# Cross-attention scores read from 32 partitions, and a PSUM copy put ahead of a square root, in a two-layer gated cross-attention and mixture-of-experts kernel

## What is computed

```python
q = _heads(nx @ W_sq + b_sq, B)              # self-attention, 16 heads of 8
...
so = _merge(_attn(q, k, v), B) @ W_so + b_so
x = x + so
nx = _ln(x, g_ln2, b_ln2)
q = _heads(nx @ W_cq + b_cq, B)              # cross-attention
k = _heads(img @ W_ck + b_ck, B)             # img has 77 rows
v = _heads(img @ W_cv + b_cv, B)
co = _merge(_attn(q, k, v), B) @ W_co + b_co
```

## Time and profile before

| | |
|---|---|
| median of 3 runs | 495.39 us (492.77, 495.39, 497.32) |
| the profiled execution | 495.81 us |
| its span, first to last instruction | 494.0 us |
| mean granted TensorE clock | 0.854 of 2.4 GHz |
| busy: PE, DVE, ACT, POOL | 357.9, 269.0, 203.0, 106.1 us |
| the seam and the cross-attention | about 265 to 335 us of the span |

### The profile page before, as it was taken

The page is one execution under the profiler, slowest core; times in us unless marked ns, Lnnn a source line. Parts: engine busy times, 40 slices in busy tenths (PEclk is TensorE's granted clock), DMA queues, the critical chain, the costliest instruction groups (busy, mean ns, idle before and its releaser), DMA issues.

```text
span 494.0 us, 5895 instructions
## 1 busy us (share of the span) xinstructions
PE 357.9 (72%) x2097; PEld 215.4 (44%) x2099; DVE 269.0 (54%) x687; ACT 203.0 (41%) x323; POOL 106.1 (21%) x144
## 2 busy tenths in 40 slices
PE   1987601995058899999997899878738986779800
PEld 1766501894023323333323485634724334569800
DVE  5235500231475998888813586444697457511366
ACT  2121200331022167777795486746333555651100
POOL 2000077001752531111110000000000356310173
PEclk9999555898567799999999699999958989899955
DMA  4692013011227564000000000009994663201132
GB/s 109 185 317 60 0 53 104 22 44 41 58 72 191 121 182 105 1 2 3 1 3 0 0 1 1 1 8 369 328 290 161 213 214 98 72 1 48 44 68 58
DMA packets 33977, 45.09 MB, mean 91 GB/s; under 512 B 5057, under 2 KB 19720, under 8 KB 33948
## 3 DMA queue, kind: packets, MB, share of 16 engines
q1 hardware_dynamic: 31132, 37.40, 25.8%
q0 software_dynamic: 2816, 7.31, 5.5%
HBM read 31.92 MB, written 12.62 MB: 90 GB/s over the span
## 4 chain that ended last, share of the span: by engine, by line
PE 56%; DVE 14%; POOL 8%; issue 8%; ACT 7%; DMA 6%; SPq 1%; POOLq 0%; DVEq 0%; ACTq 0%
PE ps L1289 8%; PE ps L1486 6%; PE ps L1474 5%; PE ps L1457 5%; POOL R L500 5%; PE ps L1765 4%; DVE mcol L1108 4%; PE ps L1724 3%; PE ps L1404 3%; PE ps L1416 3%; PE ps L1578 3%; POOL disp_d L495 2%; DMA R<-h_d,srow 2%; PE ps L1626 1%; PE ps L1587 1%
## 5 line engine op out<-in xcount | busy, mean ns | idle before, releaser
L1108 DVE TENSOR_REDUCE mcol<-ps 128x1 f32<-128x512 f32 x128 | 80.3, 683 | 6.8 <-PE ps L1457 6.5
L665 ACT ACTIVATE R<-ps 128x1024 f32<-128x1024 f32 x64 | 62.5, 1020 | 25.3 <-PE ps L1474 24.4
L1289 PE MATMUL ps<-ident,R 128*77 128x128 f32 (+1 forms) x216 | 32.4, 290 | 27.5 <-DMA R<-disp_d 24.7
L1457 PE MATMUL ps<-R 72*128 72x512 bf16 x128 | 47.0, 399 | 1.2 <-DVE mcol L1108 0.2
L500 POOL DMA_INDIRECT R<-y_d,grow x32 | 30.4, 951 | 73.5 <-DMA y_d<-R 64.3
L1289 PEld LDWEIGHTS ps<-ident,R 128*77 128x77 f32 (+1 forms) x216 | 25.3, 151 | 44.5 <-DMA R<-disp_d 25.1
L1474 PE MATMUL ps<-R 75*128 75x512 bf16 x128 | 37.6, 379 | 0.3 <-ACT R L665 0.2
L1486 PE MATMUL ps<-R,vaug 128*9 128x512 f32 x256 | 33.5, 595 | 0.6 <-ACT R L665 0.6
L557 POOL DMA_INDIRECT R<-h_d,srow x16 | 16.1, 1007 | 82.4 <-DMA h_d<-ff 74.0
L1289 PE MATMUL ps<-ident,xn 128*128 128x128 f32 x48 | 12.8, 406 | 28.7 <-issue 18.0
L1457 PEld LDWEIGHTS ps<-R 72*128 72x128 bf16 x128 | 12.8, 100 | 36.1 <-DVE mcol L1108 24.5
(11 more groups left out here) (306 smaller groups left out, 670.0 us busy)
## 6 DMA issues: line engine op xcount, KB each, us to landing
R<-in_L_ffn_W_dram SPq DMA_DIRECT2D x1, 6144.0 KB, 19.7
h_d<-R SPq DMA_DIRECT2D x12, 256.0 KB, 3.0
q_d<-R SPq DMA_DIRECT2D x24, 96.0 KB, 2.2
R<-k_d SPq DMA_DIRECT2D x24, 96.0 KB
R<-q_d SPq DMA_DIRECT2D x8, 288.0 KB
R<-in_L_ffn_w_dram SPq DMA_DIRECT2D x1, 2048.0 KB, 11.8
h_d<-ff SPq DMA_DIRECT2D x6, 256.0 KB, 2.9
y_d<-R SPq DMA_DIRECT2D x24, 44.0 KB
```

The costliest lines, as they stand in the source:

```text
L665: s.activation(probs[idx % 4], ps[:, 2 * (idx % 2):2 * (idx % 2) + 2, :].rearrange("p b t -> p (b t)"), ACT.Exp, scale=QK_SCALE).then_inc( ...
L1108: v.tensor_reduce(mcol[:, u, col:col + 1], bank(ring_bank("row", n)), AX.X, ALU.max).then_inc(s1_max, 1)
L1289: return m.transpose(dst, src, ident[0:k, 0:k])
L1457: m.matmul(bank(ring_bank("row", n)), Q9[0:KQ, b, h, t * P:(t + 1) * P], K9[0:KQ, b, h, :], start=True, stop=True).then_inc(s1_mm, 1)
```

## The change

ACT copies the transposed attention of batch 1 before the square root of batch 0 instead of behind it. And each of the score matmuls reads only the 32 partitions on which its four heads lie, in the weights (`qcT`) and in the moving operand (`kbd`): partitions 0 to 31 and 32 to 63 for the two matmuls of an even unit, 64 to 95 and 96 to 127 for those of an odd one. Since `kbd` is zero on the other partitions for these heads, the sums are the same. Outputs, banks, semaphores and the number of instructions stay as they were; the lines from 1577 on move down by up to two.

```diff
@@ ScalarE, after the self-attention
             evac_attnT(0, 0)
+            evac_attnT(0, 1)
             std_of(3, 1, [0])
-            evac_attnT(0, 1)
 
             evac_xT(3, V_LN2, [0])
             std_of(3, 1, [1])
@@ TensorE, cross_scores(un)
                 for j in range(2):
                     h = 8 * half + 4 * j
-                    ins = m.matmul(ps[:, 2 * (un % 2) + j, 0:4 * J], qcT[:, t * P:(t + 1) * P],
-                                   kbd[:, t // TB, h:h + 4, :].rearrange("p h j -> p (h j)"), start=True, stop=True)
+                    rows = slice(HD * h, HD * h + 32)
+                    ins = m.matmul(ps[:, 2 * (un % 2) + j, 0:4 * J], qcT[rows, t * P:(t + 1) * P],
+                                   kbd[rows, t // TB, h:h + 4, :].rearrange("p h j -> p (h j)"), start=True, stop=True)
                 ins.then_inc(c_mm, 1)
```

## The result

| | before | after |
|---|---|---|
| median, us | 494.08 (4 executions, 492.61 to 497.32) | **510.86** (4 executions, 507.80 to 512.87) |
| profiled execution, us (span) | 495.81 (494.0) | 512.16 (510.3) |
| mean granted clock of the profiled execution | 0.854 | 0.809 |

The changed kernel is slower: ratio 1.0325, with its 95% interval 1.0243 to 1.0407 (the two medians alone give 1.034). The forecast was 492.1 us. Where a kernel's executions fall into two groups, both are given with their counts, since these groups are what is studied.

What follows compares the result with a forecast made beforehand. PE was taken to bound the steady rounds, with DVE and ACT close behind. Gains 0.85 + 0.73 + 0.36 + 1.2 + 0.4 = 3.5 us gave 492.1 us; its own range 490.9 to 493.4, with rivals 489.4 to 495.4.

Steps and rivals of the forecast that it cites:

- The seam: 265 to 279 us, ahead of the loop: copying before the square root gains 0.85 us at the second W_cq product.
- drain behind the table load: Rival at ACT's square root: a drain follows the table load and loses 1.4 of the 3.5 us, 493.7; chance 0.03.
- The score group: Loop scores: a unit's four pieces on two row groups fill about 0.78 us instead of 1.20, rounds 1.74.
- The staggered rival: Scores: second group's first piece waits for first group's second; three streams, round 2.00 us, total 495.3; chance 0.12.
- the serial one: Rival in the scores: pieces on different row groups don't overlap; round 2.27 us, total 498.5; chance 0.08.
- Seven steady rounds: Loop, unit 0's transposes to unit 7's: each round 0.17 us shorter, 1.2 us gained.
- the clock rises later: Rival in the loop: one or two rounds at 1.2 GHz, 1.4 us more each; 493.7 to 495.0; chance 0.14.
- Unit 0's scores: First scores, at the low clock: 1.33 us on the chain instead of 2.06, gain 0.73.
- Unit 2's: Scores between unit 0's subtraction and its transposes: 0.94 us instead of 1.30, gain 0.36.
- The value rounds: Loop from unit 8 on: chain runs through value matmuls, transposes and ACT's copies, so rounds keep their old length.
- A shift of the whole tail is passed on: Everything behind the loop is bound by data, not a clock of its own, so earlier gains reach the end.
- the clock doesn't fall: Rival ahead of the loop: the earlier projection splits the idle stretch, clock stays 2.4 GHz; 490.8 us; chance 0.15.

Runs made afterwards that it cites:

- after_warm: Changed kernel plus 22 unused full-array bf16 matmuls where PE would stand idle before the loop and ahead of unit 2; 489.58 us, 0.9886.
- hybrid: Changed kernel with the scores of units 0 to 5 on all 128 partitions, the rest on 32; 492.28 us, 0.9986.
- loop_fill: Changed kernel plus four unused full-array matmuls in each of the loop's first three rounds; 497.00 us, 1.0077.
- scores_only: Changed kernel with the attnT copy back behind the square root, scores on 32 partitions; eight executions 509.71 to 515.45 us, four 492.24 to 495.08.
- seam_only: Changed kernel with scores back on 128 partitions, only the attnT copy moved; 495.92 us, 1.0052.
- switch_only: Kernel with only the copy moved, plus a one-column matmul on 32 partitions ahead of each unit's 128-partition scores; 496.30 us, 1.0053.

## Why the prediction was wrong

**The seam was right.** Times less the entry's 0.31: the root at 269.52, 0.09 behind 269.43, where 0.05 was forecast; no drain behind the table load (268.53 + 1.28, then 269.83), so that rival falls; the first `xT` at 271.66, forecast 271.6; the gap ahead of line 1138 gone; the second W_cq product 0.84 earlier, forecast 0.85.

**The score group was right at the high clock.** Four pieces fill 0.79 us (forecast 0.78), a round is 1.74 (1.74), the transposes behind are 1.10 (1.10). The staggered rival (round 2.00) and the serial one (2.27) fall: `after_warm`, `hybrid` and `loop_fill` all show 1.74.

**The step that failed** is the one under the steady rounds, "Seven steady rounds, from unit 0's transposes to unit 7's: 7 x 0.17 = 1.2", with the rounds behind it. It priced them at the high clock. In place of a gain of 0.17, each round took 1.34 us more than before, 3.25 instead of 1.91. The rival "the clock rises later" named this and sized it well: 1.4 us a round over its high-clock price, where 3.25 - 1.74 = 1.51 came. But I let it last one or two rounds with a chance of 0.14; it lasted to the last scores. I gave no reason for that bound, only that before PE ran without a break from 277.13 and had the high clock back for unit 2. In the changed kernel PE ran without a break from 281.73, and the clock stayed down. What I took from the earlier trace rows was that a full PE row brings the clock back; what these rows showed was at most that a full row of matmuls on 128 partitions does. All matmuls of that stretch are on 128 partitions, so the two could not be told apart there, and I gave that unknown no bound of its own. The range ended at 495.4 for that reason.

The Trainium skill (TensorE: Matmul & The Clock Gate, What's actually happening) says that a gate between the clock's source and the array is set by how busy PE has been of late. This trace does not agree, if busy is what PE's row of the profile shows: 61.98 of 64.60 us at 0.50, and 11.00 of 11.00 us at 1.00 in `loop_fill`.

**What the other steps came to.** Unit 0's scores, which the sum had priced at the low clock, took 1.35 us on the chain, forecast 1.33. Unit 2's were priced at the high clock and came at the low one: 1.40 instead of 1.30, a loss of 0.10 where the sum had a gain of 0.36. The value rounds were forecast to keep their length, as bound by ACT and values; at the low clock PE bound them, and they took 6.12 instead of 3.87. "A shift of the whole tail is passed on" did not hold either: 19.5 us at the end of the scores became 16.3 at the end of the span. The rival "the clock doesn't fall" did not happen: it fell at 271.4. The one mechanism that I had on the slower side, pieces one after the other, was not the one that came.

**What stays open.** Why `scores_only` had a high mean clock in four of 12 executions and the full change in none of ten: no trace of the four exists. What moves the clock at a given moment: the same instructions in the seam had 0.50 from 271.7 to 275.1 us in `hybrid`, from 272.3 to 279.0 in `seam_only`, and from 271.4 on, past the first scores, in the changed kernel, so no window of one trace settles it; the counts of executions carry the argument. Which property of the narrow scores matters, that is, the partitions or how much of the array works at a time. And why the moved copy by itself shows no gain in the median.

## What to carry to other kernels

Before a matmul is cut to fewer partitions, look at whether PE's granted clock is low where it starts: if it is, the narrow matmuls may not bring it back for a long time (54 to 82 us in the traces here), and all of PE's work there runs at half the clock, also what was not touched. If narrow matmuls are worth having, let full-array work go first (the first six units here, which took away the loss but showed no gain), or fill PE's pauses with it (0.8 to 1.1% gained, together with the moved copy), and read the granted clock in windows, beside PE's busy time, before believing any sum. A sum made of durations at 2.4 GHz needs a rival in which its whole stretch runs at 1.2.

## What was not expected of the hardware

- PE at 1.2 GHz for 64.6 us while busy for 61.98 of them, with scores on 32 of 128 partitions between transposes on all of them; on 64 partitions likewise (44.25 of 46.00 us, and low until 355.6 us). In `scores_only` it came back at 325.3 us in the middle of such scores.
- Full-array work brings it back even from there: 281 us with full scores (`switch_only`), 287 us with filler (`loop_fill`). Once high, it held through the rounds with 32 partitions in the traces of `after_warm`, `hybrid` and `loop_fill`.
- Two fp32 matmuls on different groups of 32 partitions run together: four pieces in 0.79 us, where four on the full array fill 1.20.
